# Scatters of two sorted edge lists, with and without a filling instruction between them

## The reference, cut to what matters

```
def gcn_conv(x, W, b, src, dst, num_nodes):
    h = x @ W
    loop = jnp.arange(num_nodes, dtype=src.dtype)
    s = jnp.concatenate([src, loop])
    d = jnp.concatenate([dst, loop])
    deg = jax.ops.segment_sum(jnp.ones_like(d, dtype=h.dtype), d, num_segments=num_nodes)
    dinv = jnp.where(deg > 0, jax.lax.rsqrt(deg), 0.0)
    norm = dinv[s] * dinv[d]
    msg = h[s] * norm[:, None]
    return jax.ops.segment_sum(msg, d, num_segments=num_nodes) + b

src, dst = (edge_index[0], edge_index[1])
x = gcn_conv(node_features, W1, b1, src, dst, NUM_NODES)
x = jax.nn.relu(x)
x = gcn_conv(x, W2, b2, src, dst, NUM_NODES)
```

## Time and profile before

| what | value |
|---|---|
| device time, median of 3 runs (lowest, highest) | 6540.89 us (6537.68, 6546.7) |
| time of the profiled execution | 6548.93 us |
| span of its trace | 6547.3 us |
| mean granted TensorE clock (share of full) | 0.817 |
| busy share PE / DVE / ACT / POOL | 70% / 54% / 25% / 37% |
| scatters of `back`, L555: x391 | 404.0 us busy, mean 1033 ns |
| scatters of `own`, L555: x256 | 275.9 us busy, mean 1078 ns |

### The profile page before, as it was taken

How to read it: one execution, slowest core, us unless ns; L and a number is a source line. 1 busy time by engine, 2 the same in 40 slices (tenths; PEclk the granted TensorE clock), 3 DMA queues, 4 the chain that set the end, 5 groups by cost and what they waited for, 6 DMA issues and landing times. The chain is left out here.

```text
span 6547.3 us, 89145 instructions
## 1 busy us (share of the span) xinstructions
PE 4610.8 (70%) x23040; PEld 3253.1 (50%) x23041; DVE 3512.4 (54%) x7298; ACT 1668.6 (25%) x3845; POOL 2429.1 (37%) x2714
## 2 busy tenths in 40 slices
PE   5866769734449969455657889998999495344558
PEld 1213435533347734344435577776777353344446
DVE  8988983645582345577766843342111323544543
ACT  0944543411102224011100133333222121100022
POOL 0848855555508733555520000001111201467610
PEclk8988999855559989677667989999999697677779
DMA  0002447411110038777755510003333321223210
GB/s 29 2 10 101 155 157 239 128 27 27 25 59 21 8 128 334 252 243 243 247 168 187 193 22 10 14 5 122 103 104 105 88 98 50 72 89 91 89 28 20
DMA packets 392065, 669.88 MB, mean 102 GB/s; under 512 B 115851, under 2 KB 280850, under 8 KB 387242
## 3 DMA queue, kind: packets, MB, share of 16 engines
q1 hardware_dynamic: 295938, 420.30, 19.8%
q0 software_dynamic: 95744, 247.14, 12.6%
q10 hardware_dynamic: 192, 0.15, 0.0%
HBM read 438.59 MB, written 228.81 MB: 102 GB/s over the span
## 5 line engine op out<-in xcount | busy, mean ns | idle before, releaser
L3367 POOL CAST sagel_piece<-x 128x1600 fp32r<-128x1600 f16 (+1 forms) x75 | 112.4, 1499 | 1582.4 <-DMA x<-counts 1140.0
L1072 POOL DMA_INDIRECT wsum_a_rows<-table,edge_src x416 | 426.5, 1025 | 273.5 <-issue 111.2
L1086 PE MATMUL wsum_a_ps<-wsum_a_hot,wsum_a_rows 128*128 128x128 f32 x1664 | 293.8, 352 | 330.0 <-DVE big L1113 253.7
L2172 POOL DMA_INDIRECT big<-hgt_table,edge_key x416 | 393.2, 945 | 351.0 <-DVE hgt_s_tmp L2259 200.0
L555 POOL DMA_INDIRECT back_sorted<-back_space x391 | 404.0, 1033 | 245.9 <-POOLq L1758 175.5
L1086 PEld LDWEIGHTS wsum_a_ps<-wsum_a_hot,wsum_a_rows 128*128 128x128 f32 x1664 | 275.6, 260 | 348.1 <-DVE big L1113 267.1
L3423 PE MATMUL sagel_ps<-sagel_piece,sagel_high 128*128 128x512 f32 (+1 forms) x1050 | 400.0, 388 | 0.8 <-issue 0.8
L555 POOL DMA_INDIRECT own_sorted<-big x256 | 275.9, 1078 | 311.5 <-issue 310.6
L767 PE MATMUL cnt_ps<-cnt_hot_s,cnt_hot_d 128*128 128x512 bf16 x1760 | 318.2, 334 | 94.8 <-DVE cnt_hot_s L749 89.2
L3423 PE MATMUL sagel_ps<-sagel_piece,sagel_low 128*128 128x512 f32 (+1 forms) x1050 | 380.7, 376 | 0.0
L2220 PE MATMUL hgt_s_pq<-big 128*128 x1248 | 249.0, 373 | 181.9 <-DVE hgt_s_tmp L2259 111.8
(11 more groups left out here) (977 smaller groups left out, 10887.2 us busy)
## 6 DMA issues: line engine op xcount, KB each, us to landing
hgt_edge_values<-big SPq DMA_DIRECT2D x104, 512.0 KB
big<-hgt_edge_values SPq DMA_DIRECT2D x104, 512.0 KB, 3.5
x<-counts SPq DMA_DIRECT2D x75, 400.0 KB, 3.1
x<-counts SPq DMA_DIRECT2D x75, 384.0 KB, 3.0
counts<-big SPq DMA_DIRECT2D x25, 832.0 KB
counts<-big SPq DMA_DIRECT2D x25, 768.0 KB
big<-counts SPq DMA_DIRECT2D x30, 640.0 KB
counts_turned<-big SPq DMA_DIRECT2D x30, 640.0 KB
```

Source lines behind the costliest of these rows:

```text
L1072: nc.gpsimd.indirect_dma_start(rows[n % DEEP][:, u, :], None, table, bass.IndirectOffsetOnAxis(ap=e.src[:, g:g + 1], axis=0)).then_inc(gat ...
L1086: mm = nc.tensor.matmul(ps[r.slot % 2][u][:, k * P:(k + 1) * P], rows[r.slot][:, u, k * P:(k + 1) * P], hot[r.slot % 2][:, u, :], start=Tr ...
L2172: nc.gpsimd.indirect_dma_start(rows[n % DEEP][:, u, :], None, at.table, bass.IndirectOffsetOnAxis(ap=at.index[:, g:g + 1], axis=0)).then_i ...
```

## The change

A second helper, `straight`, calls `send` without `pace`. In counts and in both convolutions it takes the place of `paced`, so the scatters there follow one another without the filling memset. The columns are also dealt out anew: `back` sends 140 in counts (100 before), 80 in convolution 1 (60), 60 in convolution 2 (45) and 111 beside experts (186), where the memset stays. `own` sends the same 98 in counts, now without memsets. So 378 scatters stand without a filler (98 of `own`, 280 of `back`), and 75 have left the experts. What is computed and what is written where is unchanged.

```
--- before.py
+++ after.py
@@ -3970,6 +3970,7 @@
                 back_space = c.enter_context(nc.sbuf_tensor("back_space", [P, n_all], F32))
                 pace = {n: c.enter_context(nc.sbuf_tensor(f"{n}_pace", [P, PACE], F32))[:] for n in ("own", "back")}
                 paced = lambda lo, hi, which: lambda pool: which.send(pool, lo, hi, pace)
+                straight = lambda lo, hi, which: lambda pool: which.send(pool, lo, hi)
                 with ExitStack() as cc:
 
                     n_own = own_dst.shape[0] // P * 5
@@ -3988,17 +3989,17 @@
                     g = gcn_first(nc, kit, A, cc, x, bufs, paced(145, 152, own_sort), paced(152, 158, own_sort))
 
                     def rest(pool):
-                        own_sort.send(pool, 158, own_sort.C, pace)
-                        back_sort.send(pool, 0, 100, pace)
+                        own_sort.send(pool, 158, own_sort.C)
+                        back_sort.send(pool, 0, 140)
                     build_counts(nc, kit, edges, counts, counts16, bufs, rest)
                     scale_and_heavy_nodes(nc, kit, g)
-                    gcn_stage(nc, kit, g, x, bufs, counts, counts16, counts_t, paced(100, 160, back_sort),
-                              paced(160, 205, back_sort))
+                    gcn_stage(nc, kit, g, x, bufs, counts, counts16, counts_t, straight(140, 220, back_sort),
+                              straight(220, 280, back_sort))
                     own_sort.fetch()
                 order.find(A["node_type_4"], c)
 
                 def send_and_order(pool):
-                    back_sort.send(pool, 205, back_sort.C, pace)
+                    back_sort.send(pool, 280, back_sort.C, pace)
                     order.write(pool)
                 gat_moe_stage(nc, kit, A, x, bufs, own, send_and_order)
             hgt_stage(nc, kit, A, x, bufs, edges, order)
```

## The result

The changed kernel took 6917.34 us (median of 4 runs, 6908.27 to 6970.91) against 6541.37 us before: a ratio of 1.0591, 95% interval 1.0536 to 1.0646. The forecast was 6920. The profiled execution has a span of 6921.5 us, 374.2 us more than before.

The account below looks back on a forecast made before the run. It took VectorE to bound counts and TensorE the convolutions, with close scatters holding back TensorE's signals. 239 + 82 + 58 = +379 us on 6548.9, less 8.0, gives 6920 us; range 6530 to 7030.

Parts of the forecast that it names:

- counts: Stage with 238 close scatters: late TensorE signals let 12 groups finish beside them, stage ends at 1178 instead of 939, +239 us.
- convolution 1: 80 close scatters, 102 us: TensorE does about a tenth of its work beside them after 8 us, +82 us.
- convolution 2: 60 close scatters, 76 us: matmuls fall to 29% of their rate, +58 us, at most 76 us.
- attention and experts: Experts: 75 pairs fewer save GpSimd 114 us, but TensorE bounds the stage, so 0; attention got no term of its own.
- stages behind: Stages after the touched ones: nothing later waits for `back` earlier than before, so 0.
- the bound from the signals: Counts beside the scatters: at 8.4 us a signal a group of 4 visits takes 33.6 us, so 9 groups get done.
- B: Only the convolutions suffer; counts escapes with scatters every 1.40 us and gains 10 us; 6671 us, chance 0.13.
- D: Signals held back half as long, 4 us each, about half the loss, +190 us; 6731 us, chance 0.11.
- C: No hold-up beside these scatters; only the missing memsets act, counts gains 10 us; 6531 us, chance 0.18.

Follow-up runs that it names:

- the third: The changed kernel unaltered, run a third time in a group with small fillers: 7011.61 us (2 runs) against 6595.7 us for the kernel before, ratio 1.0628.
- held* groups: Five groups of runs, each on one chip, where the kernel before took 6541 to 6607 us and every trace taken has remote waits.
- prompt group: One of two groups of runs where the kernel before took 6183 us and no kernel before traced there has a remote line in its waits.
- small fillers: Changed kernel plus memsets: 128 x 8 after own's and the convolutions' scatters, 128 x 160 after back's in counts; 6155.0 and 6155.35 us against 6183, 6823.86 against 6595.7.
- again, same kind: The changed kernel run again without edit: 6921.77 us against 6543.42 us for the kernel before, ratio 1.059.
- group at 6596: The group of runs on one chip where the kernel before took 6595.7 us; the changed kernel took 7011.61 us there and small fillers 6823.86 us.
- 160-column filler: Changed kernel with a memset of 128 x 160 after each scatter it had left bare: 6680.79 us against 6603.17 us for the kernel before, ratio 1.0117.
- 320 columns: Kernel before plus a 128 x 320 memset after the 25 order.write scatters and each attention gather, weighted sum bare: 6468.92 against 6607.39 us, ratio 0.979.
- prompt trace: Trace of the kernel before with a 128 x 320 memset after each of the 25 type-list scatters: 6186.38 us against 6182.93 us, ratio 1.0008.

## Why the prediction was right

**What bounds the kernel, and the mechanism.** Right in kind where it was measured: the reading of ten remote lines as signals held back by close indirect DMAs forecast new remote lines in counts and convolution 1, and they came; TensorE's busy share beside the scatters of counts fell to 16% (forecast: about 15%). The remote lines forecast at L742, L1696 and L1724 didn't come in the first trace; L1696 has one (59.9 us) in the third. In *held* groups the three measurements of the changed kernel are all slower by 5.9 to 6.3%; in a prompt group the same 378 scatters hold nothing up. The prediction took the hold-up for something that always happens, and its own trace came from a held group by luck. What makes a group held stays open: nothing I ran varies it.

**What the mechanism had wrong.** The prediction let each signal be 8.4 us late and everything go on when the last scatter is out. The 8.4 was the mean of three steps that grow, 6.30, 7.71 and 11.24 us between the four starts in the earlier trace rows; in counts the steps grow to 11.2 and stay there, the signals are 42 us late, and the queue takes 26 us to clear. What still holds is that VectorE, at most 4 visits ahead, goes at the pace of the signals. The list in the description of the kernel before was short, too: three more runs of 25 indirect DMAs (L3778, L3932, L3789) stand bare in the switch layer. No wait beside them is remote; TensorE does no matmul beside two of them, and beside the third 31 in 30 us.

**The terms**, against their measured sizes in the profiled execution:

| term | forecast | measured |
|---|---|---|
| counts | +239 | +267.6 |
| convolution 1 | +82 | +89.1 |
| convolution 2 | +58 | +28.3 |
| attention and experts | 0 | -3.0 |
| stages behind | 0 | -9.3 |
| sum (and the start, +1.5) | +379 | +374.2 |

The total is closer than its terms, and that is luck: counts is 29 us over and convolution 2 is 30 us under. Counts: the forecast was 12 groups done at 841, then 98 groups at 3.435 us. Measured were 9 groups at 870, then 101 at 3.35 (1432 matmuls in 300 us). So the longer hold-up costs 29 us, the 3 groups 10, and the faster rest gives back 8. That about 9 groups got done, as the bound from the signals said, is a second piece of luck: the first visits went through before the queue was full, and the later ones took 11.2 us each. In convolution 1 the rate that I took from the experts, 1.37 matmuls a us, agrees with the mean of 1.31 (140 in 107 us) in the same way, over a fast start and 0.36 a us at the end.

Convolution 2 is the term that was mis-sized most, and it isn't one number. Three traces of the changed kernel and one of the kernel with small fillers, with the mean distance of the 60 scatters there and the stage against its 102.3 us in the trace of before:

| run | distance, us | scatters over 1.2 us | stage longer by, us |
|---|---|---|---|
| first | 1.40 | 13 | 28.3 |
| again, same kind | 1.44 | 16 | 9.5 |
| third, in the group at 6596 | 1.33 | 6 | 58.8 |
| small fillers, in the group at 6596 | 1.40 | 4 | 63.5 |

The timeline of the first of these shows where the distance comes from:

```profile
1559.71 1.64 POOL L555 DMA_INDIRECT back_sorted<-back_space  x1 [0.30 <-issue]
...
1560.21 1.03 DVE L1724 CAST gcn_piece<-big 128x1664 fp32r<-128x1664 f16 x1 [0.74 <-PE gcn_ps L1658]
```

A scatter that meets a cast of VectorE (L1724) takes 1.64 instead of 0.97 us. As long as TensorE is prompt, VectorE keeps casting and so keeps the scatters apart; once signals are late, the casts stop and the scatters close up. That the two hold each other up in this way is argued from the table and the row; no kernel took the casts away. The mean distance alone does not decide it: the first and the last line of the table have 1.40 us and 28.3 and 63.5 us. The two large losses are both of the group at 6596, so the group is a rival that stands. My bound was 48 to 76 us, and for the first trace its lower end was too high: it went by the rate of matmuls beside scatters of 1.27 us, which these are not.

**What was excluded rightly.** Experts gained nothing from 75 pairs fewer, since GpSimd was not late there. Paced alone, the new dealing costs 36 us in counts and convolution 2; the prediction's 3 us for convolution 2 was too small, and the changed kernel doesn't pay it, since bare scatters are out in time.

**The rivals.** B (counts escapes because its scatters are stretched to 1.40 us) failed for the reason that was given against it: when VectorE waits, the scatters fall back to 1.27. With a 160-column filler the same stage does escape. D's 4 us a signal was not seen in the changed kernel. C's outcome, no loss, is what a prompt group gives, though not for C's reasons: nothing about the scatters differs there. Its gain in counts is 25 us instead of 10, since beside bare scatters a group takes 3.44 us, nearly as if there were none. The Trainium skill's rule ("SBUF — State Buffer", section "Who interferes with whom"), that only the port pair of VectorE and GpSimd contends and that PE and ACT never wait on anyone, therefore fits the prompt groups and doesn't describe the held ones, where TensorE does 136 matmuls in 300 us.

## What to carry to other kernels

Waits that the trace puts down to "remote" beside close indirect DMAs were here a hold-up of signals. Measure it from the end of the work that signalled (the program says which visit a wait is for) and not from the length of the wait: the waits here were 10 us and the signals 42 us late. Read its pace late in a burst, since the first turns are still quick, and add the time in which the queue clears. Whether the pace goes by signals or by matmuls is open. Before taking fillers out (or putting them in), see how far apart the indirect DMAs really come beside this stage's VectorE work, and measure more than once, in separate groups of runs: small fillers gave -0.5% in two groups and +3.4% in another. In held groups fillers paid in the attentions (434.1 us of gathers instead of 460.6) and gained nothing in the weighted sum; they also set a floor, 1.51 us a gather with 320 columns, so no filler is free.

## What the runs showed of the hardware that I had not expected

- The hold-up belongs to some groups of runs: the same kernel, with small fillers, has 15 remote lines in one group and none in two others (6824 against 6155 us), and the kernel before took 6541 to 6607 us in five groups and 6183 in two. Between the trace of before and the prompt trace lie 364 us, and the four stretches of indirect DMA beside TensorE make up 353 of them: 95 and 174 in the attentions' gathers, 63 in the weighted sum's, 21 in experts. This says where the time lies; that signals are the whole of its cause is shown for experts, whose 20 to 21 us the fillers give back, and not for the gathers.
- It is graded by the distance of the DMAs: 1.27 us apart, signals come through every 11.2 us in counts and are 42 us late; at 1.38 TensorE gets about 2.4 matmuls a us through convolution 1 instead of 7.4; at 1.50 waits of up to 4.4 us remain; at 1.52 beside convolution 1 no remote wait was seen, though the stage was 10 to 13 us longer in two of the held groups than in the trace of before.
- It outlasts the DMAs: in counts the signals came together only 26 us after the last scatter had ended.
- GpSimd's own semaphore updates are late too (a memset waited 0.74 us for the one before it, 1.58 us at most), while VectorE's reached TensorE in 0.13 us in the same stretch.
- It is the memsets, not the scatters, that slow VectorE in counts: 3.65 us a group beside pairs and 3.44 beside bare scatters in a prompt group.
